# Spreading step sizes in a Mamba scan: stationary and moving rows padded with zeros from 96 to 128 partitions

## The reference, cut to what matters

```
def _mamba(x, W_in, conv_w, conv_b, W_xp, W_dt, dt_b, A_log, Dp, W_out):
    xz = x @ W_in.T
    xp, z = split(xz, 2)                          # 256 channels each
    xc = silu(causal_conv(xp, conv_w) + conv_b)
    dt_lo, Bm, Cm = split(xc @ W_xp.T)            # 8, 64 and 64 wide
    dt = softplus(dt_lo @ W_dt.T + dt_b)
    A = -exp(A_log)
    def step(h, (xt, dtt, Bt, Ct)):
        dA = exp(dtt[:, :, None] * A)
        h = dA * h + (dtt * xt)[:, :, None] * Bt[:, None, :]
        return h, einsum('ben,bn->be', h, Ct)
    y = scan(step, 0, (xc, dt, Bm, Cm)) + xc * Dp
    return (y * silu(z)) @ W_out.T
x1 = _mamba(xn, ...m1)                # in the order of time
x2 = flip(_mamba(flip(xn), ...m2))    # against it
out = layernorm(x1 + x2) + xn
```

## Time and profile before

| | us |
|---|---|
| three runs | 4419.17, 4422.01, 4432.62 |
| their median | 4422.01 |
| the profiled execution | 4426.82 |
| its span, first to last instruction | 4425.0 |
| PE, DVE, ACT, POOL busy in it | 3580.8, 3278.4, 2367.4, 2500.9 |
| mean clock granted to TensorE | 0.808 of full speed |

### The profile page before, as it was taken

One profiled execution on the slowest core, in us unless ns is written; L12 is line 12 of the kernel. 1 busy time (PEld: TensorE's weight loads), 2 busy tenths in 40 slices (PEclk: granted clock), 3 DMA queues, 4 the chain that ended last, 5 costly groups with the idle time before them and its releaser, 6 DMA issues. The chain is left out here.

```text
span 4425.0 us, 81252 instructions
## 1 busy us (share of the span) xinstructions
PE 3580.8 (81%) x26013; PEld 2271.0 (51%) x26013; DVE 3278.4 (74%) x5820; ACT 2367.4 (54%) x5461; POOL 2500.9 (57%) x2256
## 2 busy tenths in 40 slices
PE   5888888888866786875879799657988986988995
PEld 3666666666644654664754577422434442444443
DVE  4777777777746855765630788588999977999995
ACT  2555555555533533542332566466666756666761
POOL 2555555555544514424310333439999955999991
PEclk6999999999977987877989899875666676566666
DMA  1000000000000000000000000027777735777760
GB/s 55 9 9 9 9 9 9 9 9 9 9 19 0 0 6 15 0 7 5 0 27 0 20 1 1 15 96 237 233 226 222 230 120 183 234 232 226 227 216 27
DMA packets 196676, 328.22 MB, mean 74 GB/s; under 512 B 96048, under 2 KB 126016, under 8 KB 194368
## 3 DMA queue, kind: packets, MB, share of 16 engines
q1 hardware_dynamic: 196288, 323.29, 23.9%
HBM read 304.30 MB, written 18.87 MB: 73 GB/s over the span
## 5 line engine op out<-in xcount | busy, mean ns | idle before, releaser
L3555 ACT ACTIVATE banks<-banks,alog 128x255 f32<-128x255 f32 x2048 | 788.2, 448 | 364.5 <-PE banks L3469 223.7
L3469 PE MATMUL banks<-dt_rows,selectors 96*128 96x510 bf16 x1024 | 507.6, 552 | 170.3 <-ACT banks L3555 95.0
L3644 DVE TENSOR_TENSOR_SCAN h<-banks,dBx 128x1024 f32<-128x1024 f32 x256 | 579.3, 2279 | 50.5 <-ACT banks L3555 47.6
L3622 POOL TENSOR_TENSOR dBx<-residual,b_by_state 128x1024 f32<-128x1024 f32 x256 | 597.4, 2354 | 33.7 <-POOLq L3615 16.6
L3622 POOL TENSOR_TENSOR norm_featmajor<-norm,b_by_state 128x1024 f32<-128x1024 f32 x256 | 597.9, 2356 | 4.7 <-DVE h L3644 2.3
L3644 DVE TENSOR_TENSOR_SCAN h<-banks,norm_featmajor 128x1024 f32<-128x1024 f32 x256 | 580.0, 2278 | 13.1 <-ACT banks L3555 8.4
L3484 PE MATMUL banks<-h,c_spread 128*32 128x128 f32 x8192 | 486.3, 379 | 10.0 <-DVE h L3644 7.8
L3484 PEld LDWEIGHTS banks<-h,c_spread 128*32 128x32 f32 x8192 | 275.3, 145 | 306.1 <-issue 256.7
L3469 PEld LDWEIGHTS banks<-dt_rows,selectors 96*128 96x128 bf16 x1024 | 139.8, 152 | 363.8 <-ACT banks L3555 275.9
L973 POOL TENSOR_TENSOR weighted<-probs,f 128x1024 f32<-128x1024 f32 x64 | 120.8, 1903 | 215.4 <-DVE f L1024 214.2
L2611 POOL TENSOR_TENSOR out_factors<-out_norms,exponents 128x4 f32<-128x4 f32 x64 | 64.5, 1008 | 288.7 <-DVE out_norms L2776 288.7
(11 more groups left out here) (451 smaller groups left out, 8847.5 us busy)
## 6 DMA issues: line engine op xcount, KB each, us to landing
residual<-mamba_dtx_rows SPq DMA_DIRECT2D x512, 256.0 KB, 3.5
norm<-mamba_dtx_rows SPq DMA_DIRECT2D x512, 256.0 KB, 3.4
mamba_dt_rows<-dt_parts SPq DMA_DIRECT2D x8, 768.0 KB, 3.4
dt_rows<-mamba_dt_rows SPq DMA_DIRECT2D x32, 192.0 KB, 4.9
delta_blocks<-A_turned SPq DMA_DIRECT2D x256, 8.0 KB, 1.5
inv_turned<-delta_blocks SPq DMA_DIRECT2D x256, 8.0 KB, 1.8
mamba_dtx_rows<-dtx SPq DMA_DIRECT2D x16, 256.0 KB, 3.6
c_spread<-in_l3a_zero SPq DMA_DIRECT2D x2, 1160.0 KB, 6.8
```

What stands on the lines that cost most here:

```text
L3469: nc.tensor.matmul(out, mem["sel"][:, row].rearrange("r n g -> r (n g)"), rows[:, kh, 2 * x:2 * x + 2, 1:], start=True, stop=True).then_in ...
L3555: e = fn(per_step(decay[l % 2])[:, 2 * x + j, 1:], k.bank[x][:, j * T + 1:(j + 1) * T], ACT.Exp, scale=mem["A"][:, at:at + 1])
L3622: nc.gpsimd.tensor_tensor(per_step(dBx[l % 4]), per_step(kept[l % 4]), across(mem["B"][:, tokens(tb)], 4), ALU.mult).then_inc(q["dbx"], 1)
L3644: v.tensor_tensor_scan(flat(h[:, u % 2, 4 * i:4 * i + 4, :]), decay[l % 2], dBx[l % 4], 0.0, ALU.mult, ALU.add).then_inc(q["scanned"], 1)
```

## The change

Both tiles get 128 rows. The 32 new rows of each are set to zero once, on POOL at the head of mamba_inputs for m = 1, with a drain behind each memset. The cast that fills selectors, and the DMAs that fill dt_rows, now name the first 96 rows. The spread's code is unchanged, since it takes whole tiles, so each of the 1024 spreads now loads 128 x 128 weights and streams 128 x 510 numbers.

```
-    m["rows"] = p.sb("dt_rows", [SROWS, 2, 4, T], BF16)
+    m["rows"] = p.sb("dt_rows", [P, 2, 4, T], BF16)
...
-    m["sel"] = p.sb("selectors", [SROWS, 16, 64, SE], BF16)
+    m["sel"] = p.sb("selectors", [P, 16, 64, SE], BF16)
...
-                    sp.dma_start(mem["rows"][:, 0], mem["dt_rows"][:, 0:4, 0:T]).then_inc(mem["rows_in"][0], 16)
+                    sp.dma_start(mem["rows"][0:SROWS, 0], mem["dt_rows"][:, 0:4, 0:T]).then_inc(mem["rows_in"][0], 16)
...
                 if m == 1:
+                    nc.gpsimd.memset(mem["sel"][SROWS:P], 0.0)
+                    pool.drain()
+                    nc.gpsimd.memset(mem["rows"][SROWS:P], 0.0)
+                    pool.drain()
                     nc.gpsimd.tensor_copy(rev[:], k.HT[:, :, PAD + T - 1:PAD - 1:-1]).then_inc(q["reversed"], 1)
...
-                    v.tensor_copy(mem["sel"][:], mem["self"][:].unsqueeze(2).to_broadcast([SROWS, 16, 64, SE]))
+                    v.tensor_copy(mem["sel"][0:SROWS], mem["self"][:].unsqueeze(2).to_broadcast([SROWS, 16, 64, SE]))
...
-                    sp.dma_start(rows[:, kh], mem["dt_rows"][:, 4 * kh:4 * kh + 4, tb * T:(tb + 1) * T]).then_inc(rows_in[kh], 16)
+                    sp.dma_start(rows[0:SROWS, kh], mem["dt_rows"][:, 4 * kh:4 * kh + 4, tb * T:(tb + 1) * T]).then_inc(rows_in[kh], 16)
```

## The result

| | median us | runs | lowest to highest |
|---|---|---|---|
| before | 4425.52 | 8 | 4419.17 to 4432.62 |
| after | 4404.29 | 8 | 4401.29 to 4414.47 |

The ratio is 0.9945, with a 95% interval of 0.993 to 0.996: 21 us faster. The forecast was 4419, its range ended at 4408, and "faster by over 0.3%" had a chance of 0.10. The profiled execution after took 4408.23 us, with a span of 4406.4 us, 18.6 less than before.

What follows compares the result with a forecast made beforehand. POOL was taken to set the scans' pace, busy 592.3 us in stretches of 607 and 604. The terms -3.4 - 2 + 0 + 2 = -3.4 us, from the median 4422.0, gave 4418.6, stated as 4419; 8-in-10 range 4408 to 4428.

Steps and rivals of the forecast that it cites:

- pairs of gaps of 0.21 and 0.36 us: POOL's gaps after 16 slow PE steps with turns; six pairs in two scans, 3.4 us, should be gone.
- term of the slow steps: In the scans, a higher clock brings PE's steps with turns mostly below 2.354 us, removing POOL's gaps: -3.4 us.
- term of the branch: At PE's loop branch the stop stays, but catching up, some 3.6 us over all branches, shrinks: -2 us.
- upper bound of 15.9 us: All POOL's waits for DVE in the two running scans, the most a better PE could give back there.
- a rival with a chance of 0.1: Whole gain: most branch waits go too and the scans' ends run at 2.4 GHz, 4406 us; chance 0.1.
- ends of the scans: Where DVE waits 16.2 us for PE's last chunks and turns: 0, bounds 2 us either side.
- The memsets: Two on POOL in the inputs of m = 1, delaying DVE's convolution: +2 us, bounds -4 and +3.7.
- the unmoved clock: Rival: TensorE's clock in the scans ignores the padding, leaving only the memsets' cost, 4424 us; chance 0.22.
- the slower case: Rival: memsets priced by elements, 3.6 us, hold DVE back while the clock gives next to nothing, 4426 us; chance 0.12.

Runs made afterwards that it cites:

- The square: POOL's loss above its pace in both scans, without DMA waits: 96 rows 21.2 us, 128 rows 3.2; with PE's loop written out, 96 rows 2.2, 128 rows 0.0.

## Why the prediction was wrong

**What held.** POOL sets the pace. The clock in the scans follows the rows, with four row counts in order (0.53, 0.63, 0.755 and 0.875); its size was guessed low, 0.7 to 0.85 where 0.87 and 0.88 were measured. A fuller PE did not go with a higher clock: with 64 rows PE was busiest, 596 of 631 us, and had the lowest clock, 0.52. The 32 rows cost the instruction nothing (376 ns at the shortest and 634 at the longest, with 96 and with 128). The pairs of gaps of 0.21 and 0.36 us are gone.

**The term of the slow steps** was -3.4 and came out as -8.4. I took the waits that the list showed for all that POOL lost. Steps of 2.48 us against a pace of 2.31 leave 0.16 us each, too small to be listed, and I had set the pace at the recorded 2.354 us, which overlaps the next product by 0.04. Sixteen steps at 0.16 are 2.6 us a batch row, or 36 us over 14 batch rows if all such steps were slow. Not all were, and the buffers hid a part; 8.4 us reached POOL.

**The term of the branch** was -2 and came out as -9.7. This is the step that failed. I wrote that "the stop itself stays", which is right (5.2 us), and took its price for POOL with it. That PE comes out of it at the low level is right too: the clock was 0.50 behind the stop at all four branches, before (3223.00 to 3229.00, 3378.00 to 3387.00, 3936.50 to 3940.00, 4090.00 to 4093.50) and after. But what a stop costs depends on how many buffers are free when it comes, and these the slow steps had used up. The square shows it: 21.2, 3.2, 2.2 and 0.0. So POOL's waits for DVE, which were to sum to about 10 us, came to 2.9. A reading was wrong as well: POOL's wait of 1.53 us in the earlier trace rows isn't PE catching up, but the second stop, here in the trace before:

```profile
3226.80 1.04 PE L3469 MATMUL banks<-dt_rows,selectors 96*128 96x510 bf16 x2 [1.83 <-issue]
```

The upper bound of 15.9 us was worked out and given to a rival with a chance of 0.1; it deserved most of the chance once the clock was expected to rise. That rival's 4406 is close to the measured 4404, but its reasons didn't hold: the stops stayed as long as they were, and DVE's waits for PE at the ends of the scans grew.

**The ends of the scans** were 0 with bounds of 2. DVE's lag behind POOL fell by 5.2 us, since DVE is closer to POOL when the last product is done, and DVE's wait for PE's tail grew by 1.6.

**The memsets** were +2 within -4 and +3.7, and cost +3.6. I counted by bytes, 0.96 us for 1024 f32; 2048 bf16 took 1.80, as 2048 f32 do (1.81). That a delay on POOL passes through DVE to the whole stage was right. The first rival, the unmoved clock, and the slower case fell with the clock.

## What to carry to other kernels

Where a trace shows TensorE's granted clock changing, here between 0.50 and 1.00, and its step is near the pace of the engine that bounds the loop, look at how many rows its matmuls use. Here 32 zero rows cost the instruction nothing (376 to 634 ns with them and without) and lifted the clock from 0.65 and 0.61 to 0.87 and 0.88, which paid up to the point where PE was off the path. Before pricing stalls one by one, ask whether they draw on the same free buffers between engines; if they do, as here, removing either can give nearly the sum. Measure the bounding engine from start to start, not by its recorded durations and listed waits.

## What the hardware showed that I had not expected

- The granted clock of the scans was higher the more rows the spread used, zeros included, and with 112 lay between that of 96 and 128: 0.53 with 64 rows, 0.63 with 96, 0.755 with 112, 0.875 with 128, at the same columns.
- At PE's loop branch a stop of some 5 us without an instruction is followed, in the first scan, by a second one of about 2 us a step later (5.13 and 1.83, 5.21 and 2.18 us before). Why there are two is open.
- With 64 rows a step at a clock of 0.50 took 0.10 us longer than with 96 (2.58 against 2.48), ahead of the spread. This is open.
- A memset of 32 x 2048 bf16 took POOL 1.80 us, as much as 128 x 2048 f32 (1.81). On DVE the trace has it as 32 x 1024 of 32 bits, with 0.91 us.
- DVE's tensor_scalar ended just behind POOL's memset, which reads nothing: 2909.22 + 1.97 = 2911.19 against 2908.72 + 2.32 = 2911.04. It is so in all six traces with this memset, 0.15 us behind in each.
